# Masks of the attention maximum: made by TensorE in PSUM in place of ScalarE tiles

## What is computed

```python
Q = _ln(h @ Wq[i], gq[i], bq[i])
K = _ln(h @ Wk[i], gk[i], bk[i])
qi, kj = Q[src], K[dst]
score = (qi * kj).sum(-1) + 0.1 * (edge_attr * qi[:, :RBF]).sum(-1) + logm[dst]
smax = jax.ops.segment_max(score, src, num_segments=N)
es = jnp.exp(jnp.minimum(score - smax[src], 20.0))
denom = jax.ops.segment_sum(es, src, num_segments=N)
alpha = es / (denom[src] + 1e-10)
m = h[dst] @ Wm[i]
aggi = jax.ops.segment_sum(alpha[:, None] * m, src, num_segments=N)
z = jnp.concatenate([h, aggi], axis=-1) @ Wu[i]
h = _ln(h + leaky(z), go[i], bo[i])
```

## Time and profile before

| what | value |
|---|---|
| time, median of 3 runs | 15181.46 us |
| span of the profiled execution | 13904.5 us |
| granted TensorE clock, mean over the span | 0.611 |
| first and last start of the maximum's instruction (L1893, 1040 of them, four passes) | 4641.9 and 10505.0 us |
| TensorE matmul busy | 11192.1 us (80%) |
| VectorE busy | 12051.1 us (87%) |
| ScalarE busy | 8510.5 us (61%) |
| GpSimd busy | 7242.8 us (52%) |

### The profile page before, as it was taken

The page is one execution under the profiler, slowest core; times in us unless marked ns, Lnnn a source line. Parts: engine busy times, 40 slices in busy tenths (PEclk is TensorE's granted clock), DMA queues, the critical chain, the costliest instruction groups (busy, mean ns, idle before and its releaser), DMA issues.

```text
span 13904.5 us, 633522 instructions
## 1 busy us (share of the span) xinstructions
PE 11192.1 (80%) x194575; PEld 9511.0 (68%) x194575; DVE 12051.1 (87%) x29601; ACT 8510.5 (61%) x28744; POOL 7242.8 (52%) x9217
## 2 busy tenths in 40 slices
PE   3799999577667899799998899898996677686576
PEld 3566666457666777687777777787776666676566
DVE  8688888588998899889998899898998889799997
ACT  0466666385776788678886788768884212167630
POOL 3577777363554555365553555365552455465446
PEclk5555555559558655595557755595555678685597
DMA  9433333766995777487775777487776966589857
GB/s 375 139 85 85 85 85 85 53 194 257 285 286 220 236 191 191 120 315 191 190 191 185 252 191 191 126 311 192 193 192 199 289 188 221 166 302 282 234 201 204
DMA packets 3519407, 2773.01 MB, mean 199 GB/s; under 512 B 2341177, under 2 KB 3123128, under 8 KB 3519018
## 3 DMA queue, kind: packets, MB, share of 16 engines
q1 hardware_dynamic: 2793946, 1087.59, 31.0%
q0 software_dynamic: 236192, 860.68, 21.3%
q10 hardware_dynamic: 489008, 821.78, 15.9%
HBM read 1656.63 MB, written 1112.41 MB: 199 GB/s over the span
## 4 chain that ended last, share of the span: by engine, by line
PE 25%; DVE 25%; DMA 14%; issue 14%; ACT 10%; SPq 5%; DVEq 5%; ACTq 1%; POOL 0%; POOLq 0%
DMA chunk_layer_rows<-arena 7%; DVE arena L1893 6%; PE ps L1202 5%; ACT arena L1033 5%; PE ps L1193 5%; DVE arena L1820 4%; DMA arena<-edge_hot_b 3%; PE ps L1326 3%; PE ps L1293 2%; PE ps L1185 2%; DVEq L110 2%; PE ps L1361 2%; DVE arena L1798 2%; DMA chunk_gated<-arena 1%; DVE small L1851 1%
## 5 line engine op out<-in xcount | busy, mean ns | idle before, releaser
L1326 PE MATMUL ps<-arena 128*128 128x49 bf16 x56160 | 2594.3, 213 | 888.1 <-DVE arena L1836 426.1
L1326 PEld LDWEIGHTS ps<-arena 128*128 128x128 fp8e4 x56160 | 2334.4, 115 | 1200.6 <-issue 1189.8
L1293 PE MATMUL ps<-block_tables,arena 128*128 128x98 bf16 (+2 forms) x56160 | 2440.4, 201 | 574.9 <-DVE arena L1806 274.3
L1293 PEld LDWEIGHTS ps<-block_tables,arena 128*128 128x128 bf16 (+1 forms) x56160 | 2216.5, 99 | 799.3 <-issue 417.4
L776 POOL COPY block_tables<-arena 128x294 bf16 (+2 forms) x2340 | 1422.6, 608 | 2200.3 <-PE ps L1293 1329.3
L969 ACT ACTIVATE arena<-ps 128x392 f32<-128x392 f32 (+1 forms) x3900 | 1710.4, 480 | 1024.3 <-PE ps L1293 625.2
L760 POOL DMA_INDIRECT arena<-chunk_layer_rows,map_a x1040 | 1051.5, 1011 | 2001.1 <-ACT arena L1033 1914.2
L1033 ACT ACTIVATE arena<-arena,small 128x49 f32<-128x49 f32 x8320 | 1997.3, 323 | 104.5 <-ACT small L1025 6.0
L737 POOL DMA_INDIRECT edge_records<-arena x1563 | 1619.9, 1036 | 625.0 <-issue 501.9
L1806 DVE TENSOR_SCALAR arena<-arena,iota_row 128x1024 bf16<-128x1024 uint8 x2080 | 1566.3, 753 | 116.5 <-PE ps L1293 67.0
L1893 DVE CUSTOM_DVE_ANT_0 arena<-ps,arena 128x1024 bf16<-128x1024 f32 x1040 | 1273.3, 1224 | 318.8 <-PE ps L1361 216.8
(11 more groups left out here) (331 smaller groups left out, 19965.2 us busy)
## 6 DMA issues: line engine op xcount, KB each, us to landing
chunk_layer_rows<-arena ACTq DMA_DIRECT2D x1040, 392.0 KB, 3.3
arena<-node_hot_a SPq DMA_DIRECT2D x1820, 128.0 KB
arena<-edge_hot_a SPq DMA_DIRECT2D x1560, 128.0 KB
chunk_gated<-arena ACTq DMA_DIRECT2D x520, 324.0 KB, 2.7
arena<-edge_records SPq DMA_DIRECT2D x1040, 160.0 KB
chunk_rows<-arena ACTq DMA_DIRECT2D x780, 196.0 KB, 1.9
arena<-edge_records SPq DMA_DIRECT2D x520, 196.0 KB
arena<-edge_hot_b SPq DMA_DIRECT2D x780, 128.0 KB
```

What stands on the lines that cost most here:

```text
L1293: last = pe.matmul(psv[:, 2 * r + j // tpb, (j % tpb) * w:(j % tpb + 1) * w], hot[:, s, j * P:(j + 1) * P], bt4[:, s, i, 0:w], start=i == ...
L1326: last = pe.matmul(to[s % 2], he4j[:, s % 4, j, :], low_part(i, s, j), start=j == 0 and i == 0, stop=j == C8 - 1 and i == 2)
```

## The change

TensorE makes the masks. For each step it adds, in banks 4 and 5, -1e30 everywhere (weights `big_off`, whose first row is -1e30 and the rest 0, times a tile of ones) and then +1e30 times the one-hot (weights `big_on`, the identity times 1e30, with the one-hot as the moving operand): 0 where the edge belongs to the node, -1e30 elsewhere. `spread_s` adds the scores on top of that. These are four matmuls of 512 columns for each step, in a new function `mask_s`, which stands in the turn between `turn_s` and `pick_max` and takes over the wait for the maximum of the step before. ScalarE's `masks` and the ring `hn4` are not used any more; its two waits and SyncE's wait for it go too. VectorE's `peak` becomes a plain maximum over 1024 columns of PSUM, with one `hold` in place of two. Three small tiles are set once in the preparation.

```diff
-            def load_node_hots(kbp_no, masked=None):
+            def load_node_hots(kbp_no):
                 def step(k, s):
                     hold(sp, "sp", (ht_used, kbp_no * NS + k - 3))
-                    if masked is not None and not (isinstance(k, int) and k < 4):
-                        hold(sp, "sp", (at["not"], masked * NS + k - 3))
                     sp.dma_start(hs4u[:, s % 4, :], hot_na[bass.ds(k * P, P), :]).then_inc(ht_loaded[s % 4], 16)
...
-                def masks(k, s):
-                    if isinstance(k, int) and k < 4:
-                        hold(act, "act", (ht_loaded[s % 4], landed(l + 1, k, s, 4)))
-                    else:
-                        hold(act, "act", (ht_loaded[s % 4], landed(l + 1, k, s, 4)), (at["gm"], base + k - 3))
-                    act.activation(hn4[:, s % 4, :], hs4[:, s % 4, :], ACT.Identity, bias=neg_big[:, 0:1], scale=BIG).then_inc(at["not"], 1)
...
-                walk(nc, act, NS, [(2, weights), (2, weigh), (1, READ), (0, masks), (1, corrected, True), (0, turn), (1, kept, True)], (ACT_ENGINE, blk_a))
+                walk(nc, act, NS, [(2, weights), (2, weigh), (1, READ), (1, corrected, True), (0, turn), (1, kept, True)], (ACT_ENGINE, blk_a))
...
+                def mask_s(k, s):
+
+                    again(pe, at["gm"], base, k, 1)
+                    for h in range(2):
+                        pe.matmul(psv[:, 4 + h, :], big_off, all_ones, start=True, stop=False, skip_group_check=True)
+                        pe.matmul(psv[:, 4 + h, :], big_on, hs4[:, s % 4, h * 512:(h + 1) * 512], start=False, stop=False, skip_group_check=True)
+
                 def spread_s(k, s):
                     r = s % 2
                     pe.wait_ge(at["ev"], base + k + 1)
-                    again(pe, at["gm"], base, k, 1)
                     for j in range(C8):
                         last = pe.matmul(psv[:, 4 + j // 4, (j % 4) * P:(j % 4 + 1) * P], sel[:, j * P:(j + 1) * P],
-                                         s_turn[:, r * P:(r + 1) * P], start=True, stop=True)
+                                         s_turn[:, r * P:(r + 1) * P], start=False, stop=True, skip_group_check=True)
                     last.then_inc(at["bc"], 1)
...
-                walk(nc, pe, NS, [add_up(l + 1, l + 1, ps_att, parts, 4), (0, pick_query), (1, turn_s), (2, pick_max), (1, spread_s)])
+                walk(nc, pe, NS, [add_up(l + 1, l + 1, ps_att, parts, 4), (0, pick_query), (1, turn_s), (1, mask_s), (2, pick_max), (1, spread_s)])
...
+            do(dve.tensor_scalar(big_on, ident[:, :], BIG, None, ALU.mult))
+            do(dve.memset(big_off, 0.0))
+            do(dve.memset(big_off[0:1, :], -BIG))
...
                 def peak(k, s):
                     r = s % 2
-                    hold(dve, "dve", (at["bc"], base + k + 1), (at["not"], base + k + 1))
-                    dve.tensor_tensor_reduce(out=junk[:, :], in0=ps[:, 4 * 512:6 * 512], in1=hn4[:, s % 4, :],
-                                             scale=1.0, scalar=-BIG, op0=ALU.add, op1=ALU.max, accum_out=gm[:, r:r + 1]).then_inc(at["gm"], 1)
+                    hold(dve, "dve", (at["bc"], base + k + 1))
+                    dve.tensor_reduce(gm[:, r:r + 1], ps[:, 4 * 512:6 * 512], AX.X, ALU.max).then_inc(at["gm"], 1)
```

More of the change, by code:

```diff
@@ L207, in build @@
         hot_n = main(4 * BT // 2, BF16)
-        junk = main(BT // 2, BF16)
+        spare = main(BT // 2)
+        junk = spare[:, 0:P // 2].bitcast(BF16)
+        all_ones = spare[:, P:P + 256].bitcast(BF16)
+        big_off = spare[:, P + 256:P + 320].bitcast(BF16)
+        big_on = spare[:, P + 320:P + 384].bitcast(BF16)
         scratch = arena[:, scratch_at:scratch_at + NB * 2 * WK]
@@ L250, in build @@
         half_pi = sb("half_pi", [P, 1])
-        neg_big = sb("neg_big", [P, 1])
         blk_of = sb("block_of_partition", [P, 2])
@@ L356, in build @@
         he4j = hot_e.bitcast(F8).rearrange("p (s j c) -> p s j c", s=4, c=P)
-        hn4 = hot_n.rearrange("p (s c) -> p s c", s=4)
         rows8g = edges(arena[:, scratch_at:], 8, WG)
@@ L433, in build @@
         at = {n: sem("att_" + n) for n in (
-            "q", "keys", "not", "prod", "red", "mid", "tr", "ev", "bc", "gm", "max", "low", "cor",
+            "q", "keys", "prod", "red", "mid", "tr", "ev", "bc", "gm", "max", "low", "cor",
             "sub", "exp", "ph")}
@@ L678, in layer @@
                 spread(l + 1, row_b)
-                walk(nc, sp, NS, [(0, load_node_hots(l * 2 + 3, l)), (0, load_edges(0, R, at["keys"], l * NS)), (2, load_edge_hots(hot_ea, l + 1))])
+                walk(nc, sp, NS, [(0, load_node_hots(l * 2 + 3)), (0, load_edges(0, R, at["keys"], l * NS)), (2, load_edge_hots(hot_ea, l + 1))])
             with sp.Fori(0, L - 1) as l:
@@ L1451, in _ @@
             dve.memset(half_pi[:, :], PI / 2).then_inc(cleared, 1)
-            dve.memset(neg_big[:, :], -BIG).then_inc(cleared, 1)
+            dve.memset(all_ones, 1.0).then_inc(cleared, 1)
             dve.memset(nul_l[0:1, :], 0.0).then_inc(cleared, 1)
```

## The result

The changed kernel takes 15539.56 us, median of four runs (15526.71 to 15547.7), beside 15179.94 us for the kernel before. The ratio is 1.0239, 95% interval 1.0226 to 1.0253: 2.4% slower, +360 us. The forecast was 15450 us with a range of 15150 to 15980, so sign and range held and the middle was 90 us low.

What follows compares the result with a forecast made beforehand. A ring through VectorE, TensorE and ScalarE was taken to set the 4.34 us attention step. 5/6 x 4.42 + 1/6 x 5.5 = 4.60 us, +270 us over 1040 steps, plus 1277 us above the span: 15450 us, range 15150 to 15980.

Steps and rivals of the forecast that it cites:

- The ring: Attention step: masks delay pick_max, on which shifted, products and peak depend; at 2.4 GHz pick_max starts at 2.97 us.
- The price of the columns: Four mask matmuls on TensorE, 2048 columns a step: 1.71 us at 1.2 GHz, 0.86 us at 2.4 GHz.
- The dearer bound: Upper price for the four mask matmuls: 2.04 us at 1.2 GHz, 1.06 at 2.4, adding 0.2 to 0.33 a step.
- The step at the upper level: Attention step with TensorE at 2.4 GHz: peak to peak taken as 4.42 us, against 4.34 before the change.
- The clock: TensorE in the attention passes: 2.4 GHz for five steps in six, otherwise 1.2 GHz at 5.5 us; chance 0.66.
- The hold: VectorE's queue before peak: one hold less, 0.12 us a step taken off, bounds 0 and 0.15.
- The step before: Attention step of the unchanged kernel: 4.34 us, from 251 maxima in 1090 us, for 1040 steps.
- The 1277 us: Median of the runs above the profiled span of 13904.5 us; taken as unchanged by the change.
- The removals: ScalarE's mask of 1.133 us a step removed: frees no time by itself, as TensorE is not ready earlier.
- Always high: Rival: TensorE at 2.4 GHz in every attention step, 4.42 us a step, 15265 us; chance 0.16.
- Always low: Rival: TensorE at 1.2 GHz in every attention step, 5.5 us a step, 16390 us; chance 0.08.
- Faster: Rival: VectorE's queue alone sets the step, shifted to peak 0.65 us, step 4.2, 15035 us; chance 0.10.

Runs made afterwards that it cites:

- idle matmuls: Changed kernel plus two 512-column matmuls per attention step that nobody reads, between pick_query and the transpose: 15414.53 us, ratio 1.0117 to the unchanged kernel.
- after: The changed kernel itself, masks on TensorE between turn_s and pick_max, against the unchanged kernel: 15539.56 us, ratio 1.0239.
- before + idle: Unchanged kernel plus four 512-column matmuls per attention step that nobody reads, between pick_query and the transpose: 15341.12 us, ratio 1.0071.
- before on the other kind of chip: Unchanged kernel profiled once more, on a chip of the kind with the short preparation: 13929.01 us, one run.
- masks ahead + idle with two holds: Changed kernel with mask_s ahead of turn_s, two unread matmuls per step and a second hold before the maximum, on the faster kind of chip: 13705.82 us, ratio 0.9847.
- masks ahead + idle: Changed kernel with mask_s ahead of turn_s and two unread 512-column matmuls per step behind pick_query: 15183.82 us, ratio 0.9966 to the unchanged kernel.
- after again: Changed kernel run again without edits, beside the unchanged kernel on the same slower kind of chip: 15629.61 us, ratio 1.0245.
- before again: Unchanged kernel profiled once more, on a chip of the slower kind with the long preparation: 15269.69 us, one run.

## Why the prediction was right, and which terms were off

- *The ring.* Right, point by point, at the upper level: pick_max at 2.98 (forecast 2.97), shifted at 3.65 (3.6), from shifted to the maximum 0.82 in the shortest steps (0.85). shifted waits for pick_max in 248 steps, and TensorE's wait for ScalarE's copy is gone. The idle matmuls show that this ring, and not the clock, holds 0.14 us a step (4.55 against 4.41) of the loss.
- *The price of the columns.* 0.21 us apart at 2.4 GHz and 0.42 at 1.2: 0.87 and 1.68 us for four, where 0.86 and 1.71 were taken. The dearer bound was not needed.
- *The step at the upper level.* The term that was mis-sized: 4.42 was taken, 0.03 under the sum of its own parts (4.45). The shortest steps are 4.47, but a good part is 4.57 or longer, the 479 steps wholly at that level have a mean of 4.54, and with the clock always up it is 4.55. One step was costed, and the spread of steps around it, which the earlier trace rows hints at with waits in a part of the steps only, was left out: 0.13 x 5/6 = 0.11 us.
- *The clock.* The forecast of a mixed clock was right in its sum, less so in its picture. Five steps in six at 2.4 GHz would be 0.80 of the time; measured are 0.76. But the steps are not of two kinds: 62% lie wholly at 2.4 GHz, 5% wholly at 1.2, and a third contain a change of level and lie between. Together the latter two add 0.22 us to the mean of the first, where 1/6 x (5.5-4.42) = 0.18 was taken: some 0.05 us a step. The clock costs after 0.21 us a step, more than the ring.
- *The hold.* 0.12 was taken and 0.12 is what the trace shows. That the plain reduction starts 0.04 us sooner behind its hold than the fused instruction was not in the sum.
- *The step before.* 4.34 was that of one kind of chip; on the kind on which the medians were taken it is 4.41 in the first three passes, which takes 0.06 off the loss. For these passes the forecast of +0.26, plus 0.11, plus 0.05, minus 0.06, gives +0.36, and 4.77 less 4.41 is what was measured. In the fourth, shorter in both kernels, it is 4.59 less 4.28. That one of three errors pointed the other way is luck; without it the middle would have been some 150 us low.
- *The 1277 us.* Taken as unchanged, which was right in its effect, for a reason that the prediction didn't have: the span shown and the median come from chips of two kinds.
- *The removals.* Costed at nothing beyond the hold, since spread_s could start earlier only if TensorE were ready; together they are worth 0.14 us a step where nothing stands in their place. The maximum by the plain reduction is no shorter: 1225 against 1224 ns.
- *The rivals.* "Always high" priced its step at 4.42 and named what speaks against it, the idle time before the transpose. With that filled the clock was always high and the kernel still 1.2% slower, at 4.55. "Always low" is what another order of the same work gives (share 0.04). "Faster" would have needed 0.65 us from shifted to the maximum; in the steps wholly at 2.4 GHz it is 0.82 at the least.

## What to carry to other kernels

Work moved from an engine with slack to TensorE costs by its place in TensorE's order: find the wait that ends last for the next engine, and put new work behind nothing that it waits for. The same change costs 2.4%, 0.4% or 11.7% by the place of its four matmuls and what that place does to the clock and to the engines' meetings, and with the clock held up +1.2%, -0.3% or -0.1%. Where added work may move a pass from one clock level to the other, forecast both levels with their own rings and test the clock by itself by filling the largest idle piece of TensorE; and before a span is compared with a median, see whether both come from the same kind of chip.

## What the runs showed of the hardware that was not expected

- The granted clock follows the order, not only the amount. Four kernels with the same added columns gave 0.90 (steps of 4.46 us), 0.88 (4.76), 0.81 (5.14, with ScalarE's masks beside) and 0.51 (6.11). A longer step thins the same work, and a lower clock lengthens the step; that this loop is what holds the last one down is a reading that fits the four, not an experiment. The length of the step is not all of it: before + idle, with as many added columns, has 0.88 at 4.44 us, as after has at 4.76.
- More matmuls made three kernels faster: two of 512 columns a step, read by nobody, took the order with pick_max ahead from 16893.89 (ratio 1.1173) to 15219.77 (0.9986).
- An instruction of VectorE on one column and two SBUF tiles lasted 0.81 instead of 0.15 us when GpSimd's 0.80 us addition had begun 0.03 us before it, in 231 of 250 steps of a stretch of that kernel (mean 724 ns of all). Instructions with one input in SBUF and one in PSUM that began during the same addition were not lengthened.
- A hold whose wait is already met takes 0.12 us of VectorE's queue, and the maximum starts later by it, though the engine is still at work on products when the first of two holds begins. Ahead of the holds the same queue reads the block's number from its table for 0.30 us, so it gets through no earlier than the engine does.
- Open: on the chips with the long preparation shifted starts later than its queue would have it. From the start of add_raised, the instruction before it, to that of shifted it is 0.18 us in most steps of before on the other kind of chip (one directly behind the other), and 0.18 too in masks ahead + idle with two holds there. On this kind it is 0.28 in before and 0.44 with masks ahead + idle (medians of 1032 steps each), though pick_max's last matmul ended some 0.5 us before shifted starts. No run tells why; it is the likeliest place of the 0.06 us by which the step of before is longer there, and of the 0.1 us by which masks ahead + idle missed its forecast.
- Two chips differ by 1047 us in the preparation and 267 us after the last attention pass for the same kernel. In after again the preparation ran mostly at 2.4 GHz, in before again on the same chip at 1.2 (the clock row of the two pages, 40 slices, after again first):

```profile
PEclk9999999999975688879899888879887658585585
```

```profile
PEclk5555555555595595558555765567555658585585
```

The first spread began at 4192.4 and 4190.2, so the time of the preparation doesn't hang on TensorE's clock here.
